# One gelu moved a slot earlier in ScalarE's hand-written order of a graph-attention and mixture-of-experts kernel

## The chip, the cores and the metric

The kernel runs on one core of one Trainium2 chip. The metric is the device time of one execution in microseconds (us), as the median of several runs.

## The reference, cut to what matters

Node features `x` (6250 x 256, fp32), 100,000 edges sorted by their target, then one graph-attention layer and one mixture-of-experts layer, each with a layer norm ahead and a residual behind:

```python
x = x + gnn(layernorm(x), edges, W, attn, W_out)     # 4 heads of 64, softmax over the edges of a target
x = x + moe(layernorm(x), router_w, w1, b1, w2, b2)  # 8 experts, the best two by softmax

for e in range(8):
    h = gelu(tokens @ w1[e] + b1[e])                 # exact gelu, 256 wide
    y = h @ w2[e] + b2[e]
    out = out + combine[:, e:e+1] * y
```

Every expert is computed for every token, and `combine` is zero outside the best two.

## The kernel before, in words

A first stage (about 270 us) builds the table of projected features and the index of edge tiles. The second stage, where the change lies, runs two pipelines in one order of work that is written out by hand for each engine.

**Edges.** The edges stand in 832 tiles of 128, in 52 batches of 16. An iteration `it` aggregates the 16 tiles of batch `it` (one TensorE product per tile into one of four PSUM banks, L1150) while the scores of batch `it + 1` are worked out. An iteration has 16 slots, `k` = 0 to 15. In each slot ScalarE evacuates a bank to `acc` (COPY, L1382) and clears the coming one (COPY, L1384); the product of tile `t` waits until the clear number `t - 2` is done (`zr`). In slot `k` = 9 ScalarE loads the table of exponentials with a small Exp (`table_of_exp`, L1395), and in slot 10 come the exponentials of the coming batch (`weigh`, L1399 to L1401), for which VectorE waits with the four `message` multiplications of slots 11 to 14 (L858). VectorE's `onehot` (L793) of slot 15 frees the scores' product of the next iteration (`d_of_edges`, L1107, slot 0), and `rescale` (L851) after it the first aggregation. At the end of the slots 3, 5, 7, 11, 13 and 15 ScalarE's queue reads eight addresses each from a small tile into registers (`addresses`, through `loads`, L659 to L664); `evacuate` of the next slot needs them.

**Blocks.** The 50 blocks of 125 nodes stand in 17 groups, 16 of three blocks and one of two. A group takes three iterations, so 48 slots, `s` = 0 to 47. TensorE computes `hidden(g, e, f)` (the first product, L1177, six matmuls into the one bank `hb`) for half `f` of expert `e`, ScalarE makes `hT` of it by `gelu` (L1408), and TensorE's `output(g, e, i)` (L1223) multiplies that by `w2`, which VectorE adds to `y` (L987). `hidden` waits for the gelu before it, since `hb` is one bank. While group `p` is in the experts, group `p + 1` is prepared (divide, out projection, norm, router), and its first two hidden products stand at the end: `hidden(p+1, 0, 0)` in slot 42, `hidden(p+1, 0, 1)` in slot 45. Then `hidden(p+1, 1, 0)` stands in slot 0 of the next group, ahead of the aggregation and the scores' product of that slot. From group 12 on, the preparation runs six slots later (`behind`), and the router's exponential (L1428) stands in slot 47 instead of slot 42.

ScalarE's gelus stand in the slots with `s % 6` in (0, 2), with a table of exceptions, `LATE`, of slots by which one is put off. In a slot ScalarE's order is: evacuate and clear; small Exp (k = 9); `weigh` (k = 10); copies of the preparation; router; gelu; addresses. Slot 42 is a slot with `k` = 10, so that its gelu would stand right behind the exponentials; `LATE` puts it off. The gelu of product 45 is the entry 44, which stands in slot 46. A Gelu after an Exp needs its table loaded: an ACT_TABLE_LOAD stands right ahead of it.

Of the kernel before, what the change touches and what calls it, by code (L numbers as in the profile page):

```python
# [22 lines left out]
def gnn_ffn_kernel(nc, x, src, dst, W, attn, W_out, rw, w1, b1, w2, b2, out):  # L23
    N, D = x.shape
    E = src.shape[0]
    H, _, DH = W.shape
    NE = rw.shape[0]
    KC = D // P
# [41 lines left out]
    with ExitStack() as ctx:  # L70
# [500 lines left out]
        with ExitStack() as st:  # L571
# [110 lines left out]
            with nc.Block() as block:  # L682
# [403 lines left out]
                def _(pe):  # L1086
# [85 lines left out]
                    def exact(out_, lhs, rhs):  # L1172
                        terms = [(lo, hi2) for (_, lo), (hi2, _) in zip(lhs, rhs)]
                        terms += [(hi, lo2) for (hi, _), (_, lo2) in zip(lhs, rhs)]
                        terms += [(hi, hi2) for (hi, _), (hi2, _) in zip(lhs, rhs)]
                        for j, (a, b_) in enumerate(terms):
                            t = T.matmul(out_, a, b_, start=j == 0, stop=j == len(terms) - 1)  # L1177
                        return t
# [169 lines left out]
                def _(act):  # L1348
# [40 lines left out]
                        A.copy(acc[:, NB - 1, :], agg_ps[:, (NB - 1) % AB, 0:ROW]).then_inc(S["ev"], 1)  # L1389

                    GELUS = [s for s in range(3 * BT) if s % 6 in (0, 2)]
                    LATE = {26: 2, 42: 2, 44: 2}

                    def table_of_exp():
                        A.activation(warm2[:, :], zc[0:1, 0:1], ACT.Exp).then_inc(S["wm"], 1)  # L1395
# [44 lines left out]
                    for it in range(-1, LAST):  # L1440
                        p, s0 = place(it)
                        for k in range(BT):
# [22 lines left out]
                            for at in GELUS:  # L1465
                                if at + LATE.get(at, 0) == s:
                                    e, f = at // 6 + 1, at % 6 // 2
# [31 lines left out]
```

## Time and profile before

| | us |
|---|---|
| median of 3 runs | 1470.1 (1469.44 to 1472.26) |
| the profiled execution's own time | 1470.98 |
| its span, first to last instruction | 1469.2 |
| TensorE busy | 1307.9 (89%) |
| VectorE busy | 1099.6 (75%) |
| ScalarE busy | 985.1 (67%) |
| GpSimd busy | 843.6 (57%) |
| mean granted TensorE clock | 0.954 of full |

In the chain of work that ended last, TensorE has 50% of the span, ScalarE 17%, VectorE 15%. A group of the second stage takes about 73.6 us.

### The profile page before, as it was taken

How to read it: one execution, taken by the hardware profiler on the slowest of the kernel's cores; microseconds unless marked ns; L12 is line 12 of the kernel's file. 1: busy time of each engine (PE TensorE's matmuls, PEld its weight loads, DVE VectorE, ACT ScalarE, POOL GpSimd, SP SyncE). 2: the span in 40 equal slices, each digit the busy share in tenths (PEclk: the TensorE clock that was granted, in tenths of full speed). 3: DMA queues.
4: the chain of work that ended last, by engine and by line, in shares of the span. 5: the costliest groups of instructions: out<-in, count | busy, mean ns of one | idle time of the engine just before them, and what ended most of it. 6: DMA issues, size and time to landing. Idle time of an engine off the chain costs nothing.

```text
span 1469.2 us, 24806 instructions
## 1 busy us (share of the span) xinstructions
PE 1307.9 (89%) x7177; PEld 1099.0 (75%) x7177; DVE 1099.6 (75%) x3059; ACT 985.1 (67%) x2522; POOL 843.6 (57%) x886
## 2 busy tenths in 40 slices
PE   5934666699999999999999999999999999999997
PEld 3722444588888888888888888887878888788886
DVE  6735765687878787878787878887887878787543
ACT  3723665577777767676767676767776878777722
POOL 1337777766666666666666666666666666660000
PEclk9965687799999999999999999999999999999999
DMA  9564654443444343434343434343434343474000
GB/s 220 153 187 130 180 160 128 120 120 109 134 111 133 108 134 110 133 107 136 105 137 106 137 104 139 104 139 104 139 103 140 104 139 104 139 91 64 4 15 18
DMA packets 89789, 174.52 MB, mean 119 GB/s; under 512 B 22471, under 2 KB 56081, under 8 KB 89625
## 3 DMA queue, kind: packets, MB, share of 16 engines
q0 software_dynamic: 40448, 111.89, 29.8%
q1 hardware_dynamic: 48103, 60.78, 13.9%
q8 instruction: 60, 0.98, 0.3%
q14 instruction: 72, 0.59, 0.1%
q10 hardware_dynamic: 1106, 0.27, 0.1%
HBM read 159.26 MB, written 14.43 MB: 118 GB/s over the span
## 4 chain that ended last, share of the span: by engine, by line
PE 50%; ACT 17%; DVE 15%; issue 5%; POOL 4%; ACTq 2%; DMA 1%; DVEq 0%; POOLq 0%
PE ob L1223 14%; PE agg_ps L1150 13%; PE hb L1177 12%; ACT agg_ps L1384 4%; POOL ring L750 4%; ACT acc L1382 4%; DVE ring L858 3%; ACT L1395 3%; PE ob L1259 3%; ACT hT L1408 2%; ACT L1408 2%; DVE oh L793 2%; DVE y L987 2%; ACTq L659 2%; PE ob L1229 1%
## 5 line engine op out<-in xcount | busy, mean ns | idle before, releaser
L750 POOL DMA_INDIRECT ring<-table,srcE x832 | 811.7, 976 | 424.0 <-issue 208.5
L1150 PE MATMUL agg_ps<-ring,oh 128*128 128x260 f32 x1664 | 517.9, 412 | 0.8 <-ACT agg_ps L1384 0.8
L1382 ACT COPY acc<-agg_ps x831 | 306.6, 369 | 222.5 <-PE agg_ps L1150 142.1
L1223 PE MATMUL ob<-w_sb,hT 128*125 128x256 f32 x1600 | 409.3, 381 | 11.1 <-DVE y L987 10.9
L1223 PEld LDWEIGHTS ob<-w_sb,hT 128*125 128x125 f32 x1600 | 295.8, 187 | 65.9 <-issue 22.0
L1384 ACT COPY agg_ps<-zc 128x260 f32 x832 | 314.7, 378 | 28.6 <-issue 2.3
L1150 PEld LDWEIGHTS agg_ps<-ring,oh 128*128 128x128 f32 x1664 | 302.0, 202 | 39.6 <-ACT agg_ps L1384 2.0
L858 DVE TENSOR_TENSOR ring<-ring,kbank 128x1024 f32<-128x1024 f32 x208 | 244.6, 1213 | 42.0 <-ACT ring L1400 41.7
L987 DVE SCALAR_TENSOR_TENSOR y<-ob,cmb,y 125x256 f32<-125x256 f32 x400 | 188.4, 474 | 56.1 <-PE ob L1223 50.9
L1408 ACT ACTIVATE hT<-hb,b_sb 128x375 f32<-128x375 f32 (+1 forms) x272 | 153.6, 565 | 111.5 <-PE hb L1177 110.7
L1177 PE MATMUL hb<-xTh,w1l 128*128 128x376 f32 (+1 forms) x544 | 182.1, 416 | 21.7 <-ACT hT L1408 21.7
L793 DVE TENSOR_TENSOR oh<-kbank,relE 128x512 f32<-128x512 f32 x208 | 140.7, 676 | 0.8
L1177 PE MATMUL hb<-xTl,w1h 128*128 128x376 f32 (+1 forms) x544 | 136.6, 332 | 0.0
L1177 PE MATMUL hb<-xTh,w1h 128*128 128x376 f32 (+1 forms) x544 | 135.8, 331 | 0.0
L1177 PEld LDWEIGHTS hb<-xTh,w1l 128*128 128x128 f32 x544 | 98.1, 190 | 49.8 <-ACT hT L1408 36.2
L1177 PEld LDWEIGHTS hb<-xTh,w1h 128*128 128x128 f32 x544 | 97.7, 189 | 0.0
L1177 PEld LDWEIGHTS hb<-xTl,w1h 128*128 128x128 f32 x544 | 97.3, 189 | 0.0
L756 POOL TENSOR_TENSOR rstd<-mv,root_ 125x3 f32<-125x3 f32 (+1 forms) x17 | 14.8, 870 | 116.2 <-DVE mv L920 116.1
L1408 ACT ACT_TABLE_LOAD x50 | 64.2, 1283 | 0.9
L485 PE MATMUL bank<-wcat,xnT 128*125 128x264 f32 x200 | 55.2, 400 | 5.0 <-DVEq L325 2.9
L807 DVE TENSOR_TENSOR_SCAN FRP<-flags,kbank 64x128 f32<-64x128 f32 x52 | 21.3, 409 | 48.8 <-PE kbank L1115 48.8
L1395 ACT ACT_TABLE_LOAD x44 | 56.5, 1283 | 0.8
(284 smaller groups left out, 1345.6 us busy)
## 6 DMA issues: line engine op xcount, KB each, us to landing
OT<-relb_d SPq DMA_DIRECT2D x52, 512.0 KB
ring<-table,srcE POOLq DMA_INDIRECT x832
y<-in_x_dram SPq DMA_DIRECT2D x50, 125.0 KB
out_dram<-y SPq DMA_DIRECT2D x50, 125.0 KB
table<-hrow SPq DMA_DIRECT2D x25, 227.5 KB
acc<-in_x_dram SPq DMA_DIRECT2D x2, 1568.0 KB
acc<-in_L_ffn_w_dram SPq DMA_DIRECT2D x1, 2048.0 KB, 12.5
w_sb<-in_L_ffn_w_dram SPq DMA_DIRECT2D x1, 2048.0 KB, 10.9
```

Source lines behind the costliest of these rows:

```text
L485: m = T.matmul(bank[2 + b % 3][0:Q, 0:WIDE], xnT[:, b % 2, k, :], wcat[:, k, :], start=k == 0, stop=k == KC - 1)
L750: pool.indirect_dma_start(out=rings[b % RING][:, k, :], out_offset=None, in_=table[:, :], in_offset=bass.IndirectOffsetOnAxis(ap=srcE[:, t ...
L793: v.tensor_tensor(oh[:, (4 * b + q) % OHQ], iota_ps.unsqueeze(1).to_broadcast([P, 4, P]), relE[:, t0:t0 + 4].unsqueeze(2).to_broadcast([P, ...
L858: v.tensor_tensor(m, m, al.to_broadcast([P, 4, H, DH]), ALU.mult).then_inc(S["msg"], 1)
L987: v.scalar_tensor_tensor(y[0:Q, u, i, :], o[0:Q, 0:D], cmb[0:Q, u, i, e:e + 1], y[0:Q, u, i, :], ALU.mult, ALU.add).then_inc(S["ya"], 1)
L1150: T.matmul(bank_of[k // 8][k % 8], oh[:, (4 * b + q) % OHQ, k % 4, :], rings[b % RING][:, k, :], start=False, stop=True, skip_group_check= ...
L1177: t = T.matmul(out_, a, b_, start=j == 0, stop=j == len(terms) - 1)
L1223: t = T.matmul(o[0:Q, 0:D], hT[:, e % 2, f, cols], w2_sb[:, e, f, :], start=f == 0, stop=f == KC - 1)
L1382: A.copy(row_of[h][k % 8], closed[h][k % 8]).then_inc(S["ev"], 1)
L1384: A.copy(coming[h][k % 8], zc[:, 0:1].to_broadcast([P, ROW])).then_inc(S["zr"], 1)
L1395: A.activation(warm2[:, :], zc[0:1, 0:1], ACT.Exp).then_inc(S["wm"], 1)
L1408: A.activation(hT[:, e % 2, f, 0:w], hb[:, 0:w], ACT.Gelu, bias=b1_sb[:, e, f:f + 1]).then_inc(S["gl"], 1)
```

## The change

The gelu of the entry 42, which is that of `hidden(p+1, 0, 0)`, stands in slot 43 instead of slot 44, behind that slot's evacuation and clear and ahead of its addresses. The two others are where they were.

```diff
                     GELUS = [s for s in range(3 * BT) if s % 6 in (0, 2)]
-                    LATE = {26: 2, 42: 2, 44: 2}
+                    LATE = {26: 2, 42: 1, 44: 2}
```

## Rows read from the trace of the kernel before

**Rows 1.** The page: the span, and TensorE's busy time.

```profile
span 1469.2 us, 24806 instructions
PE 1307.9 (89%) x7177; PEld 1099.0 (75%) x7177; DVE 1099.6 (75%) x3059; ACT 985.1 (67%) x2522; POOL 843.6 (57%) x886
```

**Rows 2.** Waits of TensorE: us in total, times, longest us.

```profile
PE hb L1177 <- ACT hT L1408: 21.7, 24, 1.5
```

**Rows 3.** The chain that ended last, one group: start us, us, what.

```profile
727.31 1.28 ACT L1408
...
729.23 1.30 PE hb L1177 x6
```

**Rows 4.** Timeline of TensorE, that group: start, us, line, operation [idle before <- releaser].

```profile
724.42 0.51 PE L1177 MATMUL hb<-xTh,w1h 128*128 128x376 f32 x2
...
726.95 1.03 PE L1223 MATMUL ob<-w_sb,hT 128*125 128x256 f32 x4
729.23 0.61 PE L1177 MATMUL hb<-xTh,w1l 128*128 128x376 f32 x2 [1.26 <-ACT hT L1408]
...
731.92 0.70 PE L1177 MATMUL hb<-xTh,w1l 128*128 128x376 f32 x2
...
733.15 0.56 PE L1107 MATMUL kbank<-d,OT 128*128 x16
```

**Rows 5.** Timeline of TensorE: the same wait in the first and last of eleven groups.

```profile
361.19 0.61 PE L1177 MATMUL hb<-xTh,w1l 128*128 128x376 f32 x2 [1.27 <-ACT hT L1408]
...
1097.53 0.61 PE L1177 MATMUL hb<-xTh,w1l 128*128 128x376 f32 x2 [1.27 <-ACT hT L1408]
```

**Rows 6.** Timeline of ScalarE, the group of rows 4, slots 43 to 46.

```profile
725.63 0.38 ACT L1384 COPY agg_ps<-zc 128x260 f32 x1
726.51 0.38 ACT L1382 COPY acc<-agg_ps  x1 [0.51 <-issue]
...
727.31 1.28 ACT L1408 ACT_TABLE_LOAD   x1
728.61 0.57 ACT L1408 ACTIVATE hT<-hb,b_sb 128x375 f32<-128x375 f32 x1
729.08 0.37 ACT L1382 COPY acc<-agg_ps  x1
729.48 0.38 ACT L1384 COPY agg_ps<-zc 128x260 f32 x1
730.37 0.38 ACT L1382 COPY acc<-agg_ps  x1 [0.51 <-issue]
...
731.09 0.57 ACT L1408 ACTIVATE hT<-hb,b_sb 128x375 f32<-128x375 f32 x1
```

**Rows 7.** Timeline of ScalarE, slots 47 and 0 of a later group.

```profile
1173.66 1.28 ACT L1428 ACT_TABLE_LOAD   x1
1174.95 0.23 ACT L1428 ACTIVATE ex<-dif 125x30 f32<-125x30 f32 x1
1175.09 0.36 ACT L1382 COPY acc<-agg_ps  x1
...
1175.87 1.28 ACT L1408 ACT_TABLE_LOAD   x1
```

**Rows 8.** Timeline of VectorE, the group of rows 4, slot 47.

```profile
730.54 0.68 DVE L793 TENSOR_TENSOR oh<-kbank,relE 128x512 f32<-128x512 f32 x1
732.37 0.44 DVE L851 TENSOR_TENSOR agg_ps<-agg_ps,sc 128x260 f32 x1 [1.15 <-issue]
```

**Rows 9.** Timeline of TensorE, group 12, slots 45 and 0.

```profile
1170.55 0.61 PE L1177 MATMUL hb<-xTh,w1l 128*128 128x376 f32 x2 [0.50 <-ACT hT L1408]
...
1174.63 0.56 PE L1107 MATMUL kbank<-d,OT 128*128 x16
```

**Rows 10.** Timeline of VectorE, group 12, slot 47.

```profile
1173.89 0.68 DVE L793 TENSOR_TENSOR oh<-kbank,relE 128x512 f32<-128x512 f32 x1
```

**Rows 11.** Timeline of TensorE, group 0, slot 45.

```profile
287.83 0.61 PE L1177 MATMUL hb<-xTh,w1l 128*128 128x376 f32 x2 [1.47 <-ACT hT L1408]
```

## The prediction

> **What bounds the kernel now.** I read the page first: TensorE is busy for 89% of the span [rows 1], so what counts is where it stands still. The table of waits then says for whom: in the stage of the change its largest wait that comes back in every group is `hidden` waiting for a gelu, 24 times, 21.7 us [rows 2]. The chain that ended last shows that one such wait is really on the path: it runs over the table load ahead of a gelu into six matmuls of `hidden` [rows 3], and before and behind it over work that hangs on TensorE. The timeline of TensorE gives the place: in slot 45 `hidden(p+1, 0, 1)` stands still for 1.26 us [rows 4], the same to 0.03 us in eleven groups but for one of 1.55 us (first and last of them: [rows 5]). The reader is to see in rows 4 that the engine had nothing left to do at 726.95 + 1.03 = 727.98, and that the product which the gelu consumes was ready at 724.42 + 0.51 = 724.93, long before the gelu's table load began at 727.31 [rows 6]. So the gelu is late by its place in the order, not by its data.
>
> **The change, step by step.** Nothing is added or removed: the same gelu of 0.57 us and the same load of 1.28 us, one slot earlier. What moves is their order against one evacuation, one clear and one reading of addresses.
>
> Step 1, the gelu of slot 43. The clear of slot 43 begins at 725.63 [rows 6]. From an evacuation to a load behind its pair is 727.31 - 726.51 = 0.80, of which the copy takes 0.40 (729.08 to 729.48), so the load follows a clear by 0.40: it now begins at 726.03, and the gelu 1.30 later (728.61 - 727.31), at 727.33. It ends at 727.90 instead of 729.18. TensorE followed the gelu's end by 0.05 (729.23), so it could go on at 727.95, where it is ready at 727.98. The wait of 1.26 us in slot 45 is gone.
>
> Step 2, the addresses of slot 43. Before, they cost 0.51 us of idle ScalarE ahead of the evacuation of slot 44, the first issue entry of [rows 6]. They now stand behind a load and a gelu. A reading behind a load is in the trace: in slot 47 of the later groups, where the addresses come after the router's load, the next evacuation begins 0.14 us after the Exp of 0.23 us has begun [rows 7]. So I cost them at nothing, under the load of 1.28 us. If that cover is missing, they would cost what they cost behind a clear, 730.37 - 729.48 = 0.89 from the gelu's start, instead of the 0.47 from a gelu to the next copy (729.08 - 728.61): 0.42 more.
>
> Step 3, what is late next. The evacuations of slots 44 to 46 and the gelu of slot 46 follow on ScalarE's queue. From the gelu at 727.33: +0.47 to the evacuation of 44 (727.80), +0.72 for a pair (730.37 to 731.09) to that of 45 (728.52), +0.40 to its clear (728.92), +0.89 over the addresses of slot 45 to the evacuation of 46 (729.81), +0.72 to the gelu (730.53), whose end is at 731.10. Before, that gelu began at 731.09: it gains 0.56 us, not 1.26. Its product would be ready in time: it starts at 727.98 and takes 1.30 [rows 3], so 729.28. `hidden(p+1, 1, 0)` of slot 0 waits for this gelu. TensorE would be there at 731.92 - 1.26 = 730.66, and may go on at 731.10 + 0.05 = 731.15. So a new wait of 0.49 us stands in slot 0, and the gain of a group is 731.92 - 731.15 = 0.77 us.
>
> Step 4, what else could hold. The clears: the aggregation of slot 47 needs the one of slot 44, which moves to about 728.2 to 728.6, and TensorE wants it at about 730.4. Margin 1.8 us, no cost. VectorE: its chain from the exponentials does not move, since they stand ahead of the change; `onehot` of slot 47 ends at 730.54 + 0.68 = 731.22 [rows 8], and the scores' product that needs it moves from 733.15 [rows 4] to 732.38. Margin 1.2 us. `rescale` stood idle for 1.15 us for the last aggregation [rows 8] and can follow. Every wait behind that hangs on TensorE, so the shift is handed on whole. GpSimd's and SP's queues are not passed by anything that moves; they wait for TensorE's counters.
>
> Step 5, the groups where it counts differently. In groups 12, 13 and 14 the wait in slot 45 is 0.50 us [rows 9]. It goes too, but there `onehot` ends at 1173.89 + 0.68 = 1174.57 [rows 10] and TensorE's scores' product begins at 1174.63 [rows 9], so it already stands against VectorE, whose work from the exponentials on does not move. Gain nothing (bounds 0 and 0.50). In groups 15 and 16 no exponentials of edges stand ahead, and no wait is there. In group 0 the wait is 1.47 us [rows 11]; I take the 0.77 us of the others (bounds 0 and 1.47).
>
> **The sum**: 11 x 0.77 + 0.77 = 9.2 us off the span of 1469.2, so 1460.0. The profiled execution took 1470.98 and stands 0.9 us above the median of the runs shown, so the median comes to 1470.1 - 9.2 = 1460.9.
>
> Rows 6 show a switch of table at 1.28 us and the gelu 0.02 us behind it, with nothing idle ahead of it. The Trainium skill (ScalarE: Activation LUTs, section "What ACT_TABLE_LOAD costs") gives the same 1283 ns for the load but adds about 1380 ns of drain for each switch. By the page a switch would take 2.66 us; as it is the same switch before and after, its rule speaks against this change only if the drain was hidden in slot 44 and is bare in slot 43, which is the third rival.
>
> **The rivals.**
> *A: the whole wait comes back.* The new wait in slot 0 does not show, because ScalarE catches up (the addresses of slot 45 also under cover). For it: rows 7 show that they can be covered. Against it: ahead of them in slot 45 stands a clear, not a load, and both issue entries of rows 6 are of that kind. Price: 11 x 1.27 + 1.47 = 15.4, with the 3 x 0.50 of the later groups 16.9; median 1453.2 to 1454.7. Chance 0.06.
> *B: the addresses of slot 43 stay bare.* Then every step behind is 0.42 later, and the gain of a group is 0.35 us: 12 x 0.35 = 4.2; median 1465.9. Against it rows 7. Chance 0.12.
> *C, slower: the load cannot start that early behind the exponentials.* Today a slot with two copies and 0.51 us idle lies between; if something is drained in it, the load would still begin at 727.31, now with the evacuation of slot 44 behind it. Then all of step 3 is 1.28 later, TensorE goes on in slot 0 at 732.43 instead of 731.92, a loss of 0.51 us a group and 12 x 0.51 = 6.1 in all: median 1476.2. It decides from a hidden pause of 0.77 us on. Against it: rows 7, where a load follows an Exp with one pair of copies between, at 1175.87, 0.69 us after the Exp's end, with no pause. Chance 0.04. By the page's drain of 1.38 us, as an estimate, a group would lose 0.61 us; rows 7 do not show such a drain.
> *D: nothing comes of it.* The shift is taken up later in the 73 us of a group by a chain that does not hang on TensorE, such as the landing of gathers or VectorE. For it: in groups 12 to 14 exactly this holds. Against it: the chain that ended last runs through TensorE in all three iterations. Price 0 to 2 us gained, median 1468 to 1470. Chance 0.08.
> That the change does not do what it says has no room: it is one entry of a table that one loop reads.
>
> **How the numbers follow.** The forecast, a gain of 7 to 11 us, has 0.70. The range reaches to B on one side and somewhat under the forecast's low end on the other, for a share of A's relief: 1457.5 to 1466.2. It leaves out A, C and D, 0.18. A measurement of this kernel can tell 0.2%, 2.9 us, from no change. Faster by more than that: forecast, A and B, 0.88; same: 0.07 of D; slower: C with a little of D for a wait that I do not see, 0.05.
>
> **What would show it.** Right: the wait of 1.26 us at L1177 in slot 45 is gone, one of about 0.5 us at the same line stands in slot 0 with the gelu of slot 46 as releaser, and the idle time of 1.15 us ahead of L851 falls to about nothing. In all, `hidden` waits for gelus some 10 us instead of 21.7. A group takes 72.8 us instead of 73.6, but the three of step 5 as long as before. The evacuation behind the moved gelu begins 0.47 us after the gelu's start; with 0.9 us it is rival B. Wrong: a gap ahead of the load in slot 43 (C), no wait in slot 0 (A), or shorter waits at L1177 with longer ones at L793, L987 or L801 (D).

## The result and the profile after

The changed kernel took 1460.41 us as the median of four runs (1458.99 to 1461.08), against 1471.18 us (1469.44 to 1473.34) for the kernel before, a ratio of 0.9925 with a 95% interval of 0.9908 to 0.9942. Forecast were 1460.9 us and a range of 1457.5 to 1466.2. The profiled execution, the fastest of the four, took 1458.99 us with a span of 1457.2.

The page of the kernel after, against [rows 1, 2]. The last line is the group of the product at L1177: busy us, mean ns of one | idle us before it, and how much of that ended with a gelu.

```profile
span 1457.2 us, 24806 instructions
PE 1306.5 (90%) x7177; PEld 1095.0 (75%) x7177; DVE 1100.9 (76%) x3059; ACT 984.1 (68%) x2522; POOL 843.1 (58%) x886
...
L1177 PE MATMUL hb<-xTh,w1l 128*128 128x376 f32 (+1 forms) x544 | 181.2, 414 | 7.0 <-ACT hT L1408 6.4
```

The same instructions, the same busy time within 1.4 us, and 12.0 us less span: what went is idle time. TensorE's waits for gelus at L1177 fell from 21.7 us to 6.4.

ScalarE in the same group as [rows 6], slots 43 to 46:

```profile
719.37 0.38 ACT L1384 COPY agg_ps<-zc 128x260 f32 x1
719.76 1.28 ACT L1408 ACT_TABLE_LOAD   x1
721.06 0.57 ACT L1408 ACTIVATE hT<-hb,b_sb 128x375 f32<-128x375 f32 x1
721.53 0.37 ACT L1382 COPY acc<-agg_ps  x1
721.93 0.38 ACT L1384 COPY agg_ps<-zc 128x260 f32 x1
722.25 0.37 ACT L1382 COPY acc<-agg_ps  x1
722.65 0.38 ACT L1384 COPY agg_ps<-zc 128x260 f32 x1
723.53 0.38 ACT L1382 COPY acc<-agg_ps  x1 [0.51 <-PE agg_ps L1150]
...
724.25 0.57 ACT L1408 ACTIVATE hT<-hb,b_sb 128x375 f32<-128x375 f32 x1
```

Read it from the clear of slot 43 at 719.37, and so do all distances below. The first gelu begins 1.69 us behind it (forecast 1.70; 2.98 before), the next evacuation 2.16 (forecast 2.17), the gelu of slot 46 4.88 (forecast 4.90; 5.46 before). The idle entry of 0.51 us ahead of the evacuation of slot 44 is gone: the addresses, which the queue passes behind the gelu, were read while the load and the gelu ran.

TensorE in that group, against [rows 4]:

```profile
720.69 1.03 PE L1223 MATMUL ob<-w_sb,hT 128*125 128x256 f32 x4
721.69 0.61 PE L1177 MATMUL hb<-xTh,w1l 128*128 128x376 f32 x2
...
724.12 0.60 PE L1150 MATMUL agg_ps<-ring,oh 128*128 128x260 f32 x2
724.87 0.61 PE L1177 MATMUL hb<-xTh,w1l 128*128 128x376 f32 x2
...
726.01 0.56 PE L1107 MATMUL kbank<-d,OT 128*128 x16
```

The wait of 1.26 us in slot 45 is gone. In slot 0 there is a gap of 0.15 us, from 724.72 to 724.87. The weight loads of the two products, of slot 45 and of slot 0, show more of their waits:

```profile
721.68 0.30 PEld L1177 LDWEIGHTS hb<-xTh,w1l 128*128 128x128 f32 x2 [0.38 <-ACT hT L1408]
...
724.87 0.30 PEld L1177 LDWEIGHTS hb<-xTh,w1l 128*128 128x128 f32 x2 [0.56 <-ACT hT L1408]
```

The scores' product begins 6.64 us behind the clear instead of 7.52, so 0.88 us earlier. This is the measure of the gain in a group: 7.52 or 7.53 in ten of the eleven groups 1 to 11 before, 6.64 to 6.67 in all eleven after. The eleventh is group 10, the one with the wait of 1.55 us. Before, it stood at 7.81, since its evacuation of slot 44 waited for its aggregation and not for the addresses, 0.28 us longer:

```profile
1021.29 0.38 ACT L1382 COPY acc<-agg_ps  x1 [0.79 <-PE agg_ps L1150]
```

After, the gelu stands ahead of that evacuation, the distance is 6.64 like the others, and group 10 gains 1.17 us.

The timeline of VectorE in the same group, against [rows 8]:

```profile
724.28 0.68 DVE L793 TENSOR_TENSOR oh<-kbank,relE 128x512 f32<-128x512 f32 x1
724.87 0.43 DVE L851 TENSOR_TENSOR agg_ps<-agg_ps,sc 128x260 f32 x1
```

The timeline of TensorE in group 12, slot 0, against [rows 9, 10]:

```profile
1162.89 0.56 PE L1107 MATMUL kbank<-d,OT 128*128 x16 [0.81 <-DVE oh L793]
```

`rescale` lost its idle 1.15 us. In group 12 the wait for the gelu is gone and one of 0.81 us for the one-hot stands at the scores' product; its distance is 7.69 us before and after.

**Where the 12.0 us came from.** The clear of slot 43 in group 0 stood at 283.11 and stands at 282.26: 0.85 us before the change can act, scatter of one execution. In group 1 the difference is 357.58 - 355.81 = 1.77, so group 0 gave 0.92. In group 12 it is 1166.94 - 1155.20 = 11.74: the eleven groups 1 to 11 gave 9.97, which is just the sum of what their distances lost: 0.85 to 0.89 in ten of them and 1.17 in group 10. In group 14 it is 1314.70 - 1302.73 = 11.97, and at the end 12.0. The change gave 0.92 + 9.97 = 10.9 us. The 0.23 us behind that fall where the distance is the same before and after, and are not shown to be its doing. The ratio says the same (0.75% of 1471 is 11.0).

### The profile page after: what moved, and what is told of

It reads as the page before. It is cut to its first block, busy times and chain, and to the rows that moved or that the text cites. A ratio compares the mean times of both kernels' runs of the same rounds, so it can differ in the third digit from the quotient of the medians.

```text
span 1457.2 us, 24806 instructions
## 1 busy us (share of the span) xinstructions
PE 1306.5 (90%) x7177; PEld 1095.0 (75%) x7177; DVE 1100.9 (76%) x3059; ACT 984.1 (68%) x2522; POOL 843.1 (58%) x886
## 4 chain that ended last, share of the span: by engine, by line
PE 54%; DVE 16%; ACT 13%; issue 5%; POOL 4%; ACTq 1%; DMA 1%; DVEq 0%; POOLq 0%
PE ob L1223 15%; PE agg_ps L1150 15%; PE hb L1177 13%; POOL ring L750 4%; ACT agg_ps L1384 3%; DVE ring L858 3%; ACT acc L1382 3%; PE ob L1259 3%; ACT L1395 2%; DVE oh L793 2%; DVE y L987 2%; ACT hT L1408 2%; PE ob L1229 1%; PE kbank L1107 1%; DVE xn L926 1%
## 5 line engine op out<-in xcount | busy, mean ns | idle before, releaser
L1150 PE MATMUL agg_ps<-ring,oh 128*128 128x260 f32 x1664 | 515.6, 410 | 1.5 <-ACT agg_ps L1384 1.5
L1384 ACT COPY agg_ps<-zc 128x260 f32 x832 | 314.6, 378 | 28.6 <-issue 2.3
L1150 PEld LDWEIGHTS agg_ps<-ring,oh 128*128 128x128 f32 x1664 | 300.0, 200 | 40.3 <-ACT agg_ps L1384 3.1
L1177 PE MATMUL hb<-xTh,w1l 128*128 128x376 f32 (+1 forms) x544 | 181.2, 414 | 7.0 <-ACT hT L1408 6.4
L1177 PE MATMUL hb<-xTl,w1h 128*128 128x376 f32 (+1 forms) x544 | 136.5, 332 | 0.0
L1177 PE MATMUL hb<-xTh,w1h 128*128 128x376 f32 (+1 forms) x544 | 135.8, 331 | 0.0
L1177 PEld LDWEIGHTS hb<-xTh,w1l 128*128 128x128 f32 x544 | 97.4, 190 | 37.8 <-ACT hT L1408 24.7
L1177 PEld LDWEIGHTS hb<-xTh,w1h 128*128 128x128 f32 x544 | 97.6, 189 | 0.0
L1177 PEld LDWEIGHTS hb<-xTl,w1h 128*128 128x128 f32 x544 | 97.2, 189 | 0.0
L1107 PE MATMUL kbank<-d,OT 128*128 x832 | 29.0, 169 | 33.5 <-DVE oh L793 20.9
```

The costliest lines, as they stand in the source:

```text
L1150: T.matmul(bank_of[k // 8][k % 8], oh[:, (4 * b + q) % OHQ, k % 4, :], rings[b % RING][:, k, :], start=False, stop=True, skip_group_check= ...
L1384: A.copy(coming[h][k % 8], zc[:, 0:1].to_broadcast([P, ROW])).then_inc(S["zr"], 1)
```

## The experiments

The theory is that of two waits: the group is first set by the first gelu of the coming group (slot 45 waits for it), and once that one is early, by ScalarE's queue up to the gelu of slot 46 (slot 0 waits for it). The rivals: only the first counts; something else holds the group; the table's load cannot follow the exponentials closely.

**A word on the chips, needed to read every number here.** The first result came from a chip on which the kernel before takes 1470 us. The experiments ran on four chips (14, 11, 9 and 8 by the numbers on record; the first has none on record, so that it is another is inferred from the times). On these the kernel before takes 1609 to 1652 us, and on the two where the changed kernel was timed beside it, 14 and 8, it is not faster. So no run below shows a total on a chip like the first. What the experiments decide, they decide by distances inside those groups in which the disturbance described further down did not fall between slot 43 and slot 0. In such groups from 1 to 11 the distances agree with the first chip's to 0.02 us; the groups 12 to 14 are treated by themselves below. There are few of them, one to two in a trace at best, so that most of these experiments rest on a single group. (The ratios of times are those on record, which are not just the quotient of the two medians given.)

### The kernel after, again

No edit, twice.

> The kernel after, once more, beside the others of this job. The theory (call it the two-wait theory: a group's time is set first by the gelu of slot 43, then by ScalarE's queue up to the gelu of slot 46) has 9 to 11 us less than before, with the groups 12 to 14 as long as before. Each of the eleven groups 1 to 11 gains 0.88 us, measured from the clear of slot 43 to the end of the hidden product in slot 0 (7.68 us before, 6.80 us in the trace after). The rival that only noise of one run was seen has the groups' times scattered.

> The kernel after, once more, on whatever chip this job gets. Where the signals of TensorE are not late: 9 to 11 us less than before, 6.64 us from the clear of slot 43 to the scores' product. Where they are late, as in the three jobs before this one: 8.4 us as in the kernel before, and a time within 5 us of it.

Measured: 1613.73 us against 1608.92, ratio 1.0027 (1.0001 to 1.0053), and on a further chip 1651.19 against 1648.94, ratio 1.0016 (0.9992 to 1.0039). The gain is not there. In the first of the two the distance to the scores' product is 8.3 to 8.6 us in ten of the groups 1 to 11, and 6.64 in the one that was not disturbed; a group takes 80.5 us on average instead of 72.7. The critical chain of a disturbed group (start us, us, what) names the piece:

```profile
419.09 0.38 ACT agg_ps L1384
419.47 1.69 another core or an unknown queue
421.16 0.02 issue
421.18 0.58 ACT hT L1408
...
421.81 1.30 PE hb L1177 x6
```

And the timeline of the same stretch, all engines:

```profile
417.62 0.51 PE L1177 MATMUL hb<-xTh,w1h 128*128 128x376 f32 x2
...
421.11 0.48 DVE L987 SCALAR_TENSOR_TENSOR y<-ob,cmb,y 125x256 f32<-125x256 f32 x1 [1.99 <-remote]
421.18 0.57 ACT L1408 ACTIVATE hT<-hb,b_sb 128x375 f32<-128x375 f32 x1 [1.72 <-remote]
```

The product for the second gelu is over at 418.13 by its record, yet the gelu begins at 421.18. VectorE, which waits for the output product of slot 45 (over at 416.87), begins at 421.11. Two engines that wait for different products of TensorE are let go within 0.07 us. By the records, the releases came 3.1 and 4.2 us late. The ends in TensorE's records are modelled, so this does not tell whether the products ended late or their signals arrived late.

### The kernel before, profiled on such a chip

No edit.

> The kernel before, unchanged, so that its trace stands beside the others of this job. On the chips of the first two jobs every kernel took about 1610 us instead of 1470: signals of TensorE reached ScalarE and VectorE up to 2 to 4 us late at the same places of nearly every group, and between the clear of slot 43 and the scores' product the order of the gelus made no difference (8.4 us with the change and 8.4 us without). If this job runs on such a chip, this trace shows the same late release in the kernel before, at 6.6 us behind the clear. On a chip without it the group takes 73.6 us and the distance is 7.53 us.

Measured: 1648.51 us, in the range of its other runs there (1645.27 to 1659.69). ScalarE's gelu of slot 46 begins 6.7 to 7.4 us behind the clear in the groups 1 to 11, where 5.46 is what its queue needs, and the scores' product stands at 8.45 to 9.13. The kernel before has the same disturbance in the same place. That gives the reading of the two: on these chips the gelu of slot 46 is let go 6.5 to 6.8 us behind the clear in most groups (7.3 to 7.4 in a few), with and without the change, and both kernels wait for them. The time saved on the way is lost in that wait. Why they are late stays open.

### Slot 42 instead of 43

The edit against the kernel before:

```diff
-                    LATE = {26: 2, 42: 2, 44: 2}
+                    LATE = {26: 2, 42: 0, 44: 2}
```

> The entry 42 is not put off at all: its gelu stands in slot 42, right behind the exponentials. Two-wait theory: the wait in slot 45 goes completely, but the addresses of slot 43 stand behind a clear again (0.51 us idle), and the gelu of slot 46 begins 5.5 us after what was the clear of slot 43, no earlier than before the change. So a wait of about 1.5 us appears in slot 0, the gain of a group is 0.26 us and the time is 1466 to 1469, clearly slower than the kernel after. Rival (only the wait in slot 45 counts, so the earlier the better): about as fast as the kernel after or faster, 1452 to 1460. Rival C of the prediction (a hidden pause between the exponentials and the load of the gelu's table): a gap of up to 1.4 us ahead of the load in slot 42, and a time above the one before.

Measured: 1610.74 us against 1608.92, ratio 0.9992 (0.9968 to 1.0017): a total that decides nothing on this chip. The undisturbed group 10 decides, ScalarE and TensorE:

```profile
1147.05 0.22 ACT L1399 ACTIVATE kbank<-arg 128x64 f32<-128x64 f32 x1
...
1147.45 0.21 ACT L1428 ACTIVATE ex<-dif 125x30 f32<-125x30 f32 x1
1147.68 1.28 ACT L1408 ACT_TABLE_LOAD   x1
1148.98 0.57 ACT L1408 ACTIVATE hT<-hb,b_sb 128x375 f32<-128x375 f32 x1
...
1150.74 0.38 ACT L1382 COPY acc<-agg_ps  x1 [0.51 <-issue]
...
1153.47 0.57 ACT L1408 ACTIVATE hT<-hb,b_sb 128x375 f32<-128x375 f32 x1
```

```profile
1149.84 0.69 PE L1177 MATMUL hb<-xTh,w1l 128*128 128x376 f32 x2
...
1152.35 0.60 PE L1150 MATMUL agg_ps<-ring,oh 128*128 128x260 f32 x2
1154.09 0.61 PE L1177 MATMUL hb<-xTh,w1l 128*128 128x376 f32 x2 [1.14 <-ACT hT L1408]
...
1155.23 0.56 PE L1107 MATMUL kbank<-d,OT 128*128 x16
```

Here the clear of slot 43 itself has moved, so I count from the first exponential (L1399), which stands 0.90 us ahead of that clear in the kernels before and after. Before, the scores' product stands at 7.53 + 0.90 = 8.43, after at 7.54, and here at 1155.23 - 1147.05 = 8.18: a gain of 0.25 us, 0.26 forecast, and 0.64 us worse than with slot 43. The wait in slot 45 is wholly gone (1149.84 follows the output product without a gap), and still the group is hardly shorter, because a wait of 1.14 us stands in slot 0 (about 1.5 was expected; why the record shows less is told under Step 3 below). That falsifies "only the wait in slot 45 counts". Of the three slots 42, 43 and 44, slot 43 gives the shortest distance: with slot 43 the load also covers the addresses, with slot 42 it does not, and the 0.51 us are back.

It also settles rival C. The load begins at 1147.68, 0.02 us after the end of the router's exponential, and the gelu 1.30 us later. A switch costs 1.30 us here with nothing hidden around it. The 2.66 us that the Trainium skill gives for every switch (ScalarE: Activation LUTs, section "What ACT_TABLE_LOAD costs"), by its drain of 1380 ns, is in none of these rows.

### The addresses ahead of the gelu

The edit against the kernel after:

```diff
+                            if s == 43:
+                                addresses(it, k)
                             for at in GELUS:
                                 if at + LATE.get(at, 0) == s:
...
-                            addresses(it, k)
+                            if s != 43:
+                                addresses(it, k)
```

> The kernel after, but the addresses of slot 43 are read ahead of the gelu instead of behind it, so that the load does not cover them. Two-wait theory: the load itself is not held, or by at most 0.5 us, depending on whether ScalarE's queue passes it on after the addresses: the gelu begins 2.18 us after the clear instead of 1.69, TensorE waits about 0.5 us in slot 45 and the gelu of slot 46 is 0.5 us later. Gain of a group 0.38 us instead of 0.88, so about 5 to 6 us slower than the kernel after, 1465 to 1467. Rival (the covered addresses brought nothing, the order of the gelu alone did): same as the kernel after.

Measured: 1609.9 us against 1608.92, ratio 0.9988 (0.996 to 1.0016), undecided. ScalarE in the undisturbed group 8, and TensorE's scores' product:

```profile
978.01 0.38 ACT L1384 COPY agg_ps<-zc 128x260 f32 x1
978.88 1.28 ACT L1408 ACT_TABLE_LOAD   x1 [0.50 <-issue]
980.18 0.57 ACT L1408 ACTIVATE hT<-hb,b_sb 128x375 f32<-128x375 f32 x1
...
983.37 0.57 ACT L1408 ACTIVATE hT<-hb,b_sb 128x375 f32<-128x375 f32 x1
```

```profile
985.14 0.56 PE L1107 MATMUL kbank<-d,OT 128*128 x16
```

The load is held by 0.50 us, the gelus begin at 2.17 and 5.36 (2.18 and 5.38 expected), and the scores' product at 7.13 instead of 6.64: 0.49 us dearer, as expected. In slot 45 the record shows no idle entry in this group, and about 0.45 us in the disturbed ones. Of the 0.88 us that the change gives a group, 0.49 come from where the addresses stand.

### The second gelu one slot earlier too

The edit against the kernel before, so that both gelus are one slot earlier:

```diff
-                    LATE = {26: 2, 42: 2, 44: 2}
+                    LATE = {26: 2, 42: 1, 44: 1}
```

> The entry 44 also goes one slot behind instead of two, so the second gelu of the coming group stands in slot 45, right behind its product, ahead of one pair of copies and of the addresses of slot 45. Two-wait theory: what is left in slot 0 is this gelu's place in ScalarE's queue. Counted from the clear of slot 43, its product ends at 3.62 us, the gelu at 4.2 instead of 5.45, TensorE does not wait for it in slot 0, and the scores' product moves from 6.64 to 6.26 us: 0.38 us more per group in 12 groups, 4 to 5 us less than the kernel after, median about 1456. Rival 1 (after the change VectorE or something else holds the group): same as the kernel after, 1460. Rival 2 (a gelu that waits for its product holds back the evacuations of slots 46 and 47, and TensorE then waits for their clears): slower than the kernel after, with waits of L1150 for L1384.

> Entry 44 one slot behind as well as entry 42. The two-wait theory counts 6.26 us from the clear of slot 43 to the scores' product, against 6.64 with the change alone and 7.53 before: a total of 12 to 15 us less than before (median 1456 to 1458) where the signals are not late, and in the three groups from 12 on nothing (7.69 us, held by VectorE). Rival 1 (VectorE holds the group after the change): no better than the change alone, 9 to 11 us. Where the signals come late, theory and rival both have nothing: within 5 us of before.

> Both entries one slot behind. Where the signals are not late, the two-wait theory has 6.26 us and 4 to 5 us less than the kernel after beside it; the rival that something else holds the group after the change has no difference between the two. Where they are late, no difference either.

Measured: 1619.09 against 1608.92, ratio 1.0046 (1.0017 to 1.0074); 1655.95 against 1652.21, 1.0029 (1.0007 to 1.005); 1656.96 against 1648.94, 1.0033 (1.001 to 1.0056). On these chips it is slightly slower than before. The two-wait theory did not have that. Rival 2 of the first expectation had it slower than the kernel after, but its sign is missing: no wait of L1150 for L1384 stands in the groups of the first trace. The one undisturbed group of 1 to 11 in the three traces, group 9 of the first run (clear of slot 43 at 1065.22):

```profile
1068.87 0.57 ACT L1408 ACTIVATE hT<-hb,b_sb 128x375 f32<-128x375 f32 x1
1069.76 0.38 ACT L1382 COPY acc<-agg_ps  x1 [0.31 <-issue]
```

```profile
1070.22 0.70 PE L1177 MATMUL hb<-xTh,w1l 128*128 128x376 f32 x2
...
1071.45 0.56 PE L1107 MATMUL kbank<-d,OT 128*128 x16
```

The gelu begins at 3.65, no wait is left in slot 0, and the scores' product stands at 1071.45 - 1065.22 = 6.23 (6.26 expected), 0.41 less than with the change alone. Group 0, in which the first gelu is later, says the same: with it at 2.46 us and the change alone the scores' product stands at 7.41 or 7.42 us, and in the three traces here, with it at 2.43 to 2.47, at 6.17 to 6.20. So the mechanism holds in this one group and in group 0. Whether it makes the whole kernel 4 us faster on a chip like the first was not measured, so it is not offered as the better version. Why it is slower on these chips stays open: the mean distance of the disturbed groups is 8.57 us against 8.40 with the change alone on one chip, but 8.64 against 8.89 on another.

### The second gelu alone

The edit against the kernel before:

```diff
-                    LATE = {26: 2, 42: 2, 44: 2}
+                    LATE = {26: 2, 42: 2, 44: 1}
```

> The kernel before, with only the entry 44 one slot earlier (second gelu in slot 45 instead of 46, the first one in slot 44 as before). Two-wait theory: TensorE waits in slot 45 for the first gelu as before (1.26 us) and did not wait in slot 0, so nothing is gained: within 2 us of the time before. Rival (the second gelu was late by itself): 4 us or more faster than before.

Measured: 1619.06 against 1611.23, ratio 1.0071 (1.0034 to 1.0109): nothing gained, but more lost than the 2 us allowed. TensorE's wait in slot 45 is 1.25 to 1.27 us in ten of the groups 1 to 11, as before. The total alone does not rule the rival out, since on these chips the change itself gains nothing either, and none of the groups 1 to 11 was undisturbed here. What speaks against it is the trace of the kernel before on the first chip: in the groups 1 to 11 the product of slot 0 has no wait there. Group 0 is an exception. It had a wait of 0.29 us in slot 0 in that trace, and here, counted from the start of its first gelu, its scores' product comes after 3.73 us instead of 4.24. Why the whole costs 8 us on this chip stays open; the groups 12 to 14 stand at 7.68 or 7.69 like the others.

### The change from group 12 on alone

The edit against the kernel after:

```diff
-                                if at + LATE.get(at, 0) == s:
+                                if at + (LATE.get(at, 0) if at != 42 or p + 1 >= 12 else 2) == s:
```

> The change for the groups from 12 on alone; the groups 0 to 11 as before. Step 5 of the prediction has nothing there, since VectorE's one-hot holds the scores' product: same as before within 1 us, with the waits of TensorE at L1177 in slot 45 (0.50 us) turned into waits at L1107 for L793. Rival (these groups gain their 0.5 us each): 1.5 us faster, which a run hardly tells, so the distances in the trace decide, from the exponentials of one iteration to the next in groups 12 to 14.

Measured: 1611.77 against 1611.23, ratio 1.0016 (0.9991 to 1.004). In groups 12 to 14 the gelu begins 1.69 us behind the clear instead of 2.98, and the scores' product stays at 7.68 to 7.69 us. Nothing is gained there.

All traces agree on what holds these groups if one counts from the first exponential of slot 42 (L1399), with which VectorE's work begins, instead of from the clear. On the first chip the clear stands 0.78 us behind it, so the scores' product stands at 8.47 or 8.48, before and after. In some traces of the chips 8 and 9 an evacuation held the clear until 1.8 us behind the exponential. Measured from the clear the distance falls to 6.68 us there, but from the exponential it is 8.46 to 8.48, in each trace with the first gelu in slot 43 and with whole messages.

### VectorE's cover taken away in groups 12 to 14

```diff
-                        m = ring4[b % RING][:, 4 * q:4 * q + 4, :, 0:DH]
+                        w = 16 if b in (43, 46, 49) else DH
+                        m = ring4[b % RING][:, 4 * q:4 * q + 4, :, 0:w]
```

and the same width in the multiplication, once on the kernel before and once on the kernel after. Only a quarter of the message columns of these three batches is weighted.

> The kernel before, but in the three batches whose exponentials stand in slot 42 of groups 12, 13 and 14 the message multiplication covers 16 of 64 columns, so VectorE has some 3 us less in those slots (part of the messages is left unweighted). Step 5: the scores' product no longer stands against the one-hot. On its own this gives at most 0.2 us a group, since without the change TensorE is held by the gelu of slot 44 (0.50 us wait stays).

> The kernel after with the same shortened messages. If VectorE was what took the gain in groups 12 to 14, these groups are now 0.5 to 0.9 us shorter than with the shortened messages alone, and no wait for L793 stands at L1107. If they are as long as in the run beside it, something else than VectorE holds them.

Measured: one execution each, 1608.71 and 1617.64 us, totals that compare nothing. The distances of groups 12 to 14: 7.52, 7.53, 7.52 without the change and 6.66, 6.92, 6.64 with it. TensorE of group 12 with the change:

```profile
1310.18 0.62 PE L1178 MATMUL hb<-xTh,w1l 128*128 128x376 f32 x2 [0.16 <-ACT hT L1409]
...
1311.33 0.56 PE L1108 MATMUL kbank<-d,OT 128*128 x16
```

The lines are one further than in the other kernels. The wait for the one-hot is gone, and the distance (clear at 1304.67) is that of the groups below 12. So it was VectorE that kept a gain of 0.6 to 0.9 us from each of these groups. Without the change the short messages alone gave 0.17 us (7.69 to 7.52), within the 0.2 expected.

## Why the prediction was right

**Step 1** (the gelu of slot 43 at 727.33, 1.70 behind the clear): 1.69 measured, the wait of slot 45 gone.

**Step 2** (the addresses cost nothing under the load): the evacuation came 0.47 us after the gelu's start, and put ahead of the gelu the addresses cost 0.49 us a group. Rival B is out.

**Step 3** (what is late next): the right wait in the right place, but the gain was mis-sized. I had the product of slot 0 at 5.52 behind the clear, measured 5.50, and took the gain as 731.92 - 731.15 = 0.77. The term that failed is 731.92. It is the start of a product that stands queued behind another: in the kernel before it takes 733.15 - 731.92 = 1.23 us to the scores' product, and a product that starts after a wait takes 726.01 - 724.87 = 1.14. Starts of the two kinds are not comparable; the distance to the next product that is queued in both traces is, and it gives 0.88. The new wait itself was sized rightly, and the trace hides it. Queued products overlap in the records: in the kernel before the one of slot 0 begins at 731.92, 0.25 us behind the start of the aggregation ahead of it and 0.35 us ahead of that one's modelled end:

```profile
731.67 0.60 PE L1150 MATMUL agg_ps<-ring,oh 128*128 128x260 f32 x2
```

After, the aggregation begins at 724.12 and the product at 724.87, so 0.75 us behind: 0.50 us later than when queued, though the idle entry says 0.15. With slot 42 it is the same: 1154.09 is 1.74 us behind 1152.35, so 1.49 us of delay stand behind an idle entry of 1.14. That is also why all waits for gelus at L1177 come to 6.4 us and not to the some 10 that were to be seen. At the scores' product the new wait costs 0.38 us: without it the distance would be 7.52 - 1.26 = 6.26, and the kernel with both gelus early shows 6.23.

**Step 4** (what else could hold): `rescale` followed, no wait for clears came up, and the shift was handed on whole: the 9.97 us that the groups 1 to 11 gave are the sum of what their distances lost.

**Step 5** (nothing in groups 12 to 14): the distance stayed at 7.69 us, shown as VectorE's doing by the two kernels with short messages. Group 0 gave 0.92 us where 0.77 stood; it was not like the others, with a wait of 0.29 us in slot 0 already before the change. Group 10 gave 1.17 where 0.77 stood: its longer wait of 1.55 us was read, but not followed to its cause.

**The sum**: 12 x 0.77 = 9.2 us were forecast. Ten groups at 0.88, group 10 at 1.17 and group 0 at 0.92 make 10.9. That the median came out within 0.5 us of the forecast is partly luck: the forecast took 1470.1 for the kernel before, three runs, and with a fourth it is 1471.18. So it started 1.1 us too low and took off 1.6 us too little.

**What the prediction missed**: that its sum holds only where TensorE's releases come on time. Its traces had no sign of another case, and rival D, a chain that takes up the shift, had 0.08. On the two other chips where it was timed again something of that kind did take it all.

## What to carry to other kernels

An engine's wait for a late instruction is worth its length only up to the next wait of the same pair: follow the releaser's queue to its next product before writing down the gain. Where register loads and a table load stand in one queue, put the register loads behind the table load: here that was 0.49 of 0.88 us. Compare two traces of TensorE by products that are queued in both, not by the start of one that waited, and do not take its idle entry for the whole wait: 0.15 us of idle time stood for 0.50 of delay.

## What the runs showed that was not expected

The same program took 1470 us on one chip and 1609 to 1652 us on four others. The instructions are the same and TensorE's busy time is 1306.5 against 1356.0 us in the kernel after; the other 102 of the 151 us more of span (1608.6 against 1457.2) are idle time, much of it with no releaser in the profile. Some 51 us of the 151 are lost ahead of group 0's clear of slot 43, which stands at 333.55 instead of 282.26, so the first stage is hit as well. ScalarE's waits of the first of these runs, of a kind that the first chip does not have (us in total, times, longest us):

```profile
ACT acc L1382 <- remote: 69.2, 14, 30.0
...
ACT xTh L1422 <- remote: 28.1, 13, 2.9
ACT hT L1408 <- remote: 17.5, 11, 1.7
```

They fall at the same slots of nearly every group below 12 (gelu of slot 46; cast of the preparation), in each of the twelve traces taken there, and where I followed one, the waiting instruction stood behind a product of TensorE that was over by its record. What holds the releases, TensorE itself or their way, no run tells. A change of 0.7% on one chip was not there on the two others on which the same kernel was timed again, so such a change should be timed on more than one.
